# Local-attention layers of a decoder: another order of steps within each head-pair slot, on four engines

## The chip, the cores and the metric

The program runs on 1 core of one Trainium2 chip. The metric is the device time of one execution, in microseconds. Five engines work on it, each through its own list of instructions in order, and wait for one another by semaphores: TensorE (PE in the rows; PEld is its weight load), VectorE (DVE), ScalarE (ACT), GpSimd (POOL) and SyncE (SP), which here only issues DMAs.

## The reference, cut to what matters

The program is a decoder of many sublayers on x of 4 x 512 x 128. The change touches the last sublayer alone, six layers of local attention with a gated feed-forward part, in float32:

```python
for i in range(DEPTH):                                   # 6
    x = attn_layer(shift_tokens(x), Wqkv[i], ...) + x    # 16 heads of 64
    x = ffn_layer(shift_tokens(x), ln_g[i], ...) + x
# attn_layer
q = l2norm(q) * qs; k = l2norm(k) * ksc                  # per head
q = q * cos * scale + rotate_half(q) * sin * scale       # k likewise with 1/scale
out = local_attention(q, k, v)     # window 32: own block and the one before, masked softmax
return out.reshape(b, n, INNER) @ Wo
# ffn_layer
xn = (x - mu) / jnp.sqrt(var + 1e-05) * g + bln
a, gate = jnp.split(xn @ W1 + b1, 2, -1)
return a * gelu(gate) @ W2 + b2
```

## The kernel before, in words

The function is `local_attention_layers_3`. It walks through 6 layers x 4 batch rows = 24 batches, and each batch through 8 pairs of heads (`hp` 0 to 7): 192 **slots**. A slot with number n is one turn of the loop in each engine's `batch`. All loops are unrolled, and what stands in the four `batch` functions is the order in which each engine works; no scheduler moves it. The slots are pipelined: in slot n an engine works on pairs n+2, n+1, n and n-1 at different stages.

The stages of one pair m, with the functions that do them:

- `qk` (PE, L3031): queries and keys of 512 tokens, 8 matmuls, in two halves j = 0 and 1 into banks 0 and 3. The first half waits until ScalarE is done with the first head's exponentials (`exps`) two pairs earlier, since bank 0 also holds that head's scores.
- `square_part` (ACT, L3232), a half each; then `rotate` (DVE, L3363 and L3366) on the same half, which waits for that half's square; `norms` (DVE, L3375), `floor_norms` (DVE), `inverse_norms` (ACT, L3238 Ln and L3241 Exp), `add_parts` (POOL, L2975), `normalise` (DVE, L3395).
- `turn_qk` (PE, L3047 and L3050): transposes of the normalised queries (bank 6) and keys (bank 7); `copy_qT` and `copy_kT` (ACT, L3251 and L3255) take them to SBUF.
- `direct` (PE, L3076 and L3084): the mask and the scores, into banks 0 (first head) and 2 (second head). It waits for both copies, for the previous pair's exponentials, and for the square and the rotation of the half of the following pair that lies in bank 0.
- `maxima` (DVE, L3403), `exps` (ACT, L3263, 8 activations with sums into `loc_by_query`), `inverse_sums` (DVE, L3388), `divide_probs` (POOL, L2982).
- `turn_probs` (PE, L3063 and L3064): transposes of the probabilities into banks 4 and 5. It waits for `divide_probs`, and until VectorE has taken the previous pair's output out of the same banks (`heads_out`, L3411). `exps` of the next pair waits until `turn_probs` has read `loc_by_query`.
- `project_v` (PE, L3039) and `copy_v` (ACT, L3247); `copy_probs` (ACT, L3273); `values` (PE, L3105), the output of the pair in banks 4 and 5.

The feed-forward part of batch k-1 is spread over the slots of batch k. On PE it stands at the end of a slot: `project_out` in slots 0 and 1 (4 matmuls of 512 columns each time, L3115), `turn_shifted` in 2, `turn_z` in 3, `hidden` for the gate in 4 and for the other half in 5 (3 matmuls each, L3138), `feed_back` in 6 (3 matmuls, L3146). ScalarE's and VectorE's steps (`add_out`, `lower_middle`, `copy_tokens`, `token_stats`, `normal_tokens`, `copy_z`, `gelus` with two table loads, `gated`, `new_state`) stand at the end of their slots too, except `normal_tokens`. PE's steps use banks 7, 6 and 1 beside the pair's own work; before `turn_qk` PE waits, in slots 1 to 7, for the step that frees such a bank.

Of the kernel before, what the change touches and what calls it, by code (L numbers as in the profile page):

```python
# [2839 lines left out]
def local_attention_layers_3(nc, g, io):  # L2840
# [17 lines left out]
    with ExitStack() as stack:  # L2858
# [68 lines left out]
        with nc.Block() as block:  # L2927
# [43 lines left out]
            def _(pool):  # L2971
# [31 lines left out]
                def batch(k, f):  # L3003
                    for hp in range(HP):
                        n = k * HP + hp
                        if hp == LAST:
                            by_block(k + 2)
                        prepare(n + 2)
                        divide_probs(n + 1)
                        if hp == 2 and f is not None:  # L3010
                            inverse_spread(f)
# [4 lines left out]
                divide_probs(0)  # L3016
# [6 lines left out]
            def _(pe):  # L3023
# [126 lines left out]
                def batch(k, f):  # L3150
# [3 lines left out]
                    for hp in range(HP):  # L3154
# [7 lines left out]
                        qk(n + 2, next_qk, 1)  # L3162
                        if f is not None and hp == 1:
                            pe.wait_ge(s["y_half_done"], f + 1)
# [4 lines left out]
                        if f is not None and hp == 4:  # L3169
                            pe.wait_ge(s["zT_copied"], f + 1)  # L3170
                        if f is not None and hp == 5:
                            pe.wait_ge(s["gelu_done"], f * NC + NC)
                        if f is not None and hp == 6:
                            pe.wait_ge(s["inner_done"], f * NC + NC)
                        if f is not None and hp == LAST:
                            pe.wait_ge(s["y_done"], f + 2)
                        turn_qk(n + 1)
                        turn_probs(n)
                        if hp == LAST:
                            pe.wait_ge(s["xv_done"], k + 2)  # L3180
                        project_v(n + 1, next_v)
                        direct(n + 1)
                        values(n, u)
                        if f is not None:
# [4 lines left out]
                            if hp == 3:  # L3189
                                turn_z(f)  # L3190
                            if hp == 4:
# [3 lines left out]
                            if hp == 5:  # L3195
                                pe.wait_ge(s["v_copied"], n + 2)
                                hidden(f, A_BANKS, 0, "a_ready")
                            if hp == 6:
# [16 lines left out]
                f = BATCHES - 1  # L3215
                pe.wait_ge(s["v_copied"], BATCHES * HP + 1)
# [4 lines left out]
                turn_z(f)  # L3221
                hidden(f, GATE_BANKS, INNER, "gate_ready")
# [5 lines left out]
            def _(act):  # L3228
# [6 lines left out]
                def inverse_norms(m, j):  # L3235
                    part = slice(8 * j, 8 * j + 8)
                    act.wait_ge(s["floored_done"], m * 2 + (j + 1))
                    nc.scalar.activation(norm_log[:, part], floored[:, part], ACT.Ln).then_inc(s["norm_log_done"], 1)  # L3238
                    act.wait_ge(s["norm_log_done"], m * 2 + (j + 1))
                    when(act, "rotated_done", m * 2 + (j - 1))  # L3240
                    nc.scalar.activation(inv_norm[:, part], norm_log[:, part], ACT.Exp,  # L3241
                                         scale=-0.5).then_inc(s["inverse_done"], 1)
# [14 lines left out]
                def exps(m):  # L3257
                    when(act, "probs_turned", m * 2)
                    for h in range(2):
                        act.wait_ge(s["max_done"], m * 2 + (h + 1))  # L3260
                        for t in range(QT):
                            r, at = t // 2, (t % 2) * 2 + t // 2
                            nc.scalar.activation(by_query[:, h, :, t % 2, r, :],  # L3263
                                                 score_banks[h][:, t * 2 * BLOCK:(t + 1) * 2 * BLOCK].rearrange(
                                                     "p (w k) -> p w k", w=2), ACT.Exp,
                                                 bias=minus_max[:, t, h:h + 1],
# [448 lines left out]
```

## Time and profile before

| what | value |
|---|---|
| three runs | 5072.9, 5081.94 and 5083.23 us, median 5081.94 |
| the profiled execution's own time | 5055.95 us |
| its span, first to last instruction | 5054.2 us |
| granted TensorE clock, mean | 0.836 of full |
| local layers: first `qk` matmul | at 3010.7 us |
| DVE busy in them, 4000 to 4100 us | 79.5 of 100 us |
| ACT, PE, POOL busy there | 77.0, 86.1, 51.9 of 100 us |

The page gives the busy time of each engine over the whole span (PE 3786.9 us, DVE 3245.7, ACT 2783.0, POOL 1469.9). For the change only the last two fifths count, from about 3010 us on. The way to read them is slot by slot: which instruction waits, for whom, and whether that one was working or waiting itself. The last chain that the page prints covers only the closing transposes after the local layers.

### The profile page before, as it was taken

What the parts mean: (1) busy time and instruction counts of PE and PEld (TensorE: products, weight loads), DVE (VectorE), ACT (ScalarE), POOL (GpSimd) and SP (SyncE); (2) the same over time, 40 slices, a digit from 0 to 9 for tenths busy, and PEclk for the clock granted to TensorE, in tenths of its full rate; (3) what the DMA queues carried; (4) which work ended last, traced back from release to release, by engine and by line L of the source; (5) the groups of instructions that cost most, each with busy time, mean ns of one, the idle gap of its engine ahead of it and who ended that gap; (6) DMA issues with size and microseconds to landing.
All of it is one profiled execution on the core that took longest, in us unless ns stands there. A gap on an engine that the chain in (4) does not pass through costs nothing. (4 is left out here: it accounts for less than half of the span.)

```text
span 5054.2 us, 96137 instructions
## 1 busy us (share of the span) xinstructions
PE 3786.9 (75%) x32669; PEld 2234.6 (44%) x32898; DVE 3245.7 (64%) x6512; ACT 2783.0 (55%) x7830; POOL 1469.9 (29%) x2402
## 2 busy tenths in 40 slices
PE   2004767995758995886996668888888888888886
PEld 1003333333342222443442336666666666666664
DVE  8996445444328786425555328778777878787775
ACT  2034623442536785441224438777777777777775
POOL 0011202331111111110001235545454545454453
PEclk6556877556778987887997779999999999999998
DMA  1001123102114310203450000000000000000000
GB/s 45 0 0 33 35 76 68 42 11 41 27 34 101 78 27 12 59 10 96 137 140 25 1 24 29 5 9 24 5 28 5 9 24 5 9 24 5 28 5 11
DMA packets 139048, 170.17 MB, mean 34 GB/s; under 512 B 34607, under 2 KB 121755, under 8 KB 137412
## 3 DMA queue, kind: packets, MB, share of 16 engines
q1 hardware_dynamic: 138158, 164.06, 13.4%
q8 instruction: 260, 4.26, 0.4%
q14 instruction: 198, 1.62, 0.1%
q0 software_dynamic: 432, 0.23, 0.0%
HBM read 124.06 MB, written 32.89 MB: 31 GB/s over the span
## 5 line engine op out<-in xcount | busy, mean ns | idle before, releaser
L854 DVE TENSOR_REDUCE minus_max<-banks 128x1 f32<-128x512 f32 (+4 forms) x1152 | 622.0, 572 | 452.9 <-PE banks L664 440.9
L771 ACT ACTIVATE probs<-banks 128x512 f32<-128x512 f32 (+4 forms) x1152 | 613.8, 559 | 406.8 <-PE banks L632 397.4
L2982 POOL TENSOR_TENSOR loc_by_query<-loc_by_query,loc_inv_sums 128x512 f32<-128x512 f32 x386 | 469.6, 1235 | 559.5 <-DVE loc_inv_sums L3388 559.5
L2975 POOL TENSOR_TENSOR loc_cos_part<-loc_cos_part,loc_sin_part 128x512 f32<-128x512 f32 x388 | 487.8, 1276 | 412.9 <-DVE loc_sin_part L3366 412.3
L3263 ACT ACTIVATE loc_by_query<-banks,loc_minus_max 128x128 f32<-128x128 f32 x1544 | 540.5, 374 | 13.2 <-DVE loc_minus_max L3403 12.7
L3031 PE MATMUL banks<-loc_w_qkv,loc_shifted 128*128 128x256 f32 x1552 | 410.9, 412 | 169.4 <-ACT loc_by_query L3263 155.7
L632 PE MATMUL banks<-q_stack,k_stack 51*128 51x512 bf16 (+4 forms) x1152 | 438.9, 427 | 39.3 <-DMA q_stack<-max_rows 37.2
L664 PE MATMUL banks<-k_stack,q_stack 48*128 48x512 bf16 (+5 forms) x1536 | 437.1, 346 | 30.1 <-PEq L68 19.4
L3031 PEld LDWEIGHTS banks<-loc_w_qkv,loc_shifted 128*128 128x128 f32 x1552 | 307.9, 204 | 282.2 <-issue 230.0
L705 PE MATMUL banks<-probs,pair_rows 128*32 128x256 f32 (+1 forms) x4352 | 396.9, 446 | 9.5 <-issue 9.3
L3363 DVE TENSOR_TENSOR loc_cos_part<-banks,loc_table 128x512 f32<-128x512 f32 x388 | 265.3, 684 | 126.2 <-ACT loc_square L3232 125.2
L3263 ACT ACTIVATION_READ_ACCUMULATOR loc_by_query<-banks,loc_minus_max 128x1 f32 x1544 | 331.2, 215 | 0.0
L1365 ACT ACTIVATE gated<-banks 128x512 f32<-128x512 f32 x168 | 100.3, 597 | 336.2 <-PE banks L1326 336.2
L3232 ACT ACTIVATE loc_square<-banks 128x512 f32<-128x512 f32 x388 | 225.2, 604 | 106.8 <-PE banks L3031 106.1
L2028 PE MATMUL banks<-identity,srt_b 128*128 128x128 f32 x64 | 11.2, 320 | 344.6 <-DVE srt_b L2299 344.6
L3395 DVE TENSOR_TENSOR loc_rotated<-loc_cos_part,loc_inv_norm 128x512 f32<-128x512 f32 x388 | 267.2, 689 | 1.1 <-issue 0.6
L206 POOL TENSOR_SCALAR fin_shifted<-fin_moments 128x4 f32<-128x4 f32 x48 | 12.0, 249 | 870.4 <-DVE fin_moments L306 868.0
L3366 DVE TENSOR_TENSOR loc_sin_part<-banks,loc_table 128x512 f32<-128x512 f32 x388 | 264.0, 681 | 0.0
L3375 DVE TENSOR_REDUCE loc_norm_sq<-loc_square 128x8 f32<-128x512 f32 x388 | 246.1, 676 | 0.0
L1385 DVE TENSOR_TENSOR product<-gated,banks 128x512 f32<-128x512 f32 x168 | 115.7, 689 | 199.0 <-PE banks L1328 198.9
L632 PEld LDWEIGHTS banks<-q_stack,k_stack 51*128 51x128 bf16 (+1 forms) x1152 | 101.2, 97 | 284.1 <-issue 112.0
L3388 DVE RECIPROCAL loc_inv_sums<-loc_sums 128x4 f32<-128x4 f32 x386 | 68.7, 178 | 235.4 <-ACT loc_by_query L3263 235.4
(492 smaller groups left out, 8711.8 us busy)
## 6 DMA issues: line engine op xcount, KB each, us to landing
expert_share<-limited_rows SPq DMA_DIRECT2D x136, 256.0 KB, 4.1
expert_w<-in_L_ffn_pairs_dram SPq DMA_DIRECT2D x84, 192.0 KB, 2.4
q_stack<-q_pieces SPq DMA_DIRECT2D x38, 384.0 KB, 6.4
loc_w_qkv<-in_L_ffn_Wqkv_dram SPq DMA_DIRECT2D x7, 1536.0 KB, 8.0
expert_share<-grouped_rows SPq DMA_DIRECT2D x32, 256.0 KB, 4.0
k_stack<-k_pieces SPq DMA_DIRECT2D x20, 384.0 KB, 9.0
q_pieces<-q_parts SPq DMA_DIRECT2D x19, 384.0 KB, 2.6
q_stack<-max_rows SPq DMA_DIRECT2D x384, 3.0 KB
```

The source lines that it names most:

```text
L632: nc.tensor.matmul(t_bank(n, k, e)[:, q0:S], k_stack[rows_e, k0:k0 + P], q_stack[rows_e, q0:S], start=not mask, stop=True, skip_group_chec ...
L664: ins = nc.tensor.matmul(d_bank(n, k, i)[:, at * nk:at * nk + keys], q_stack[rows_e, q * P:(q + 1) * P], k_stack[rows_e, 0:keys], start=pl ...
L705: ins = nc.tensor.matmul(o_bank[at:at + COLS, lo:hi], pair_rows[quad % 2][u][:, k, e, :], probs_of(2 * quad + u, k, e)[:, lo:hi], start=(k ...
L771: nc.scalar.activation(probs_of(n, k, e)[0:kn, q0:S], t_bank(n, k, e)[0:kn, q0:S], ACT.Exp, scale=scale).then_inc(s["exp_done"], 1)
L854: nc.vector.tensor_reduce(minus_max[:, n % 2, 1 - i, qs[0]:qs[0] + len(qs)], view, AX.X, ALU.max, negate=True).then_inc(s["max_done"], 1)
L2975: nc.gpsimd.tensor_tensor(cos_part[:, tiles, :], cos_part[:, tiles, :], sin_part[:, tiles, :], ALU.add).then_inc(s["summed"], 1)
L2982: nc.gpsimd.tensor_tensor(seen, seen, inv_sums[:, h, :].unsqueeze(1).unsqueeze(3).to_broadcast([P, 2, QT, BLOCK]), ALU.mult).then_inc(s["p ...
L3031: ins = nc.tensor.matmul(g.bank[3 * j][:, (t % 2) * QK:(t % 2 + 1) * QK], xs[:, t * P:(t + 1) * P], w_qkv[:, ds(at, QK)], start=True, stop ...
L3263: nc.scalar.activation(by_query[:, h, :, t % 2, r, :], score_banks[h][:, t * 2 * BLOCK:(t + 1) * 2 * BLOCK].rearrange("p (w k) -> p w k", ...
L3363: nc.vector.tensor_tensor(cos_part[:, tiles, :], g.bank[3 * j][:, :].rearrange("p (t d) -> p t d", t=2), table[:, 0, tiles, :], ALU.mult). ...
L3366: nc.vector.tensor_tensor(sin_part[:, tiles, :].rearrange("p t (e two d) -> p (t e) two d", two=2, d=half), src, table[:, 1, tiles, :].rea ...
L3395: nc.vector.tensor_tensor(groups(rotated[:, tiles, :]), groups(cos_part[:, tiles, :]), inv_norm[:, part].unsqueeze(2).to_broadcast([P, 8, ...
```

## The change

Each engine's `batch` gets another order, and some helpers are cut differently:

- PE: `project_v(n+1)` moves ahead of the waits and of `turn_qk(n+1)`; `values` works on pair n-1 and stands ahead of `direct(n+1)`; `turn_probs(n)` stands behind `direct(n+1)`, at the end of the pair's work. The feed-forward steps from `turn_z` on move one slot later, and the waits before `turn_qk` with them.
- ACT: the slot begins with `copy_probs(n-1)`; the second half's square moves behind `copy_qT` and `copy_kT` (in slot 6 it stands ahead of `gelus`); `exps` is called for each head alone, with one `inverse_norms` on all 16 columns between the two, in place of two on 8 columns each. `copy_tokens`, `copy_z` and `gelus` stand between the first square and `copy_qT` in slots 3, 5 and 6.
- DVE: the slot begins with `inverse_sums(n, 0)`, both `normalise(n+1)` and `inverse_sums(n, 1)`; then `rotate(n+2)`, the first `norms`, `heads_out(n-1)`, the first head's `maxima(n+1)`, the second `norms`, one `floor_norms` on 16 columns in place of two, and the second head's `maxima`. `add_out`, `normal_tokens` and `new_state` stand behind `normalise`, `gated` ahead of it, `token_stats` and the tables of the next layer at the end of the slot.
- POOL: `divide_probs(n)` stands ahead of `prepare(n+2)`; before it was `divide_probs(n+1)` behind it.

The core of the diff (PE and the two engines' loops):

```diff
                         qk(n + 2, next_qk, 0)
                         qk(n + 2, next_qk, 1)
+                        if hp == LAST:
+                            pe.wait_ge(s["xv_done"], k + 2)
+                        if f is not None and hp == 6:
+                            pe.wait_ge(s["gelu_done"], f * NC + 1)
+                        if f is not None and hp == LAST:
+                            pe.wait_ge(s["inner_done"], f * NC + 1)
+                        project_v(n + 1, next_v)
...
                         turn_qk(n + 1)
+                        if n > 0:
+                            values(n - 1, 1 - u)
+                        direct(n + 1)
                         turn_probs(n)
-                        if hp == LAST:
-                            pe.wait_ge(s["xv_done"], k + 2)
-                        project_v(n + 1, next_v)
-                        direct(n + 1)
-                        values(n, u)
...
-                            if hp == 4:
+                            if hp == 5:
                                 pe.wait_ge(s["pack_loaded"], (f // B) * 16 + 16)
                                 pe.wait_ge(s["v_copied"], n + 2)
                                 hidden(f, GATE_BANKS, INNER, "gate_ready")
...
+                        if n > 0:
+                            copy_probs(n - 1)
                         square_part(n + 2, 0)
-                        square_part(n + 2, 1)
+                        if f is not None and hp == 3:
+                            copy_tokens(f)
+                        if f is not None and hp == 5:
+                            copy_z(f)
+                        if f is not None and hp == 6:
+                            square_part(n + 2, 1)
+                            gelus(f)
                         copy_qT(n + 1)
                         copy_kT(n + 1)
-                        copy_probs(n)
+                        if f is None or hp != 6:
+                            square_part(n + 2, 1)
                         copy_v(n + 1, 1 - u)
...
-                        inverse_norms(n + 2, 0)
-                        inverse_norms(n + 2, 1)
-                        exps(n + 1)
...
+                        exps(n + 1, 0)
+                        inverse_norms(n + 2)
+                        exps(n + 1, 1)
```

**ScalarE, one slot of batch 0, before.** `loc_square` is the square of a half, `loc_by_query` the exponentials, `loc_probs` the turned probabilities' copy.

```order
L3263 ACTIVATE loc_by_query,loc_sums<-banks,loc_minus_max 128x2x64 x8
L3232 ACTIVATE loc_square<-banks 128x512 x2
L3251 ACTIVATE loc_qT<-banks 128x512
L3255 ACTIVATE loc_kT<-banks 128x512
L3273 ACTIVATE loc_probs<-banks 128x384 x2
L3247 ACTIVATE loc_v_1<-banks 128x512
```

The same engine and slot now:

```order
L3266 ACTIVATE loc_by_query,loc_sums<-banks,loc_minus_max 128x2x64 x4
L3276 ACTIVATE loc_probs<-banks 128x384 x2
L3238 ACTIVATE loc_square<-banks 128x512
L3255 ACTIVATE loc_qT<-banks 128x512
L3259 ACTIVATE loc_kT<-banks 128x512
L3238 ACTIVATE loc_square<-banks 128x512
L3251 ACTIVATE loc_v_1<-banks 128x512
```

The second square moved from ahead of the two copies of turned queries and keys to behind them.

**VectorE, one slot of batch 0, before.**

```order
L3411 COPY loc_headsT<-banks 128x512
L3363 TENSOR_TENSOR loc_cos_part<-banks,loc_table 128x512
L3366 TENSOR_TENSOR loc_sin_part<-banks,loc_table 128x512
L3363 TENSOR_TENSOR loc_cos_part<-banks,loc_table 128x512
L3366 TENSOR_TENSOR loc_sin_part<-banks,loc_table 128x512
L3375 TENSOR_REDUCE loc_norm_sq<-loc_square 128x8 x2
L3382 TENSOR_SCALAR loc_floored<-loc_norm_sq 128x8 x2
L3403 TENSOR_REDUCE loc_minus_max<-banks 128x4 x2
L3395 TENSOR_TENSOR loc_rotated<-loc_cos_part,loc_inv_norm 128x512
```

The same engine and slot now:

```order
L3367 TENSOR_TENSOR loc_cos_part<-banks,loc_table 128x512
L3370 TENSOR_TENSOR loc_sin_part<-banks,loc_table 128x512
L3367 TENSOR_TENSOR loc_cos_part<-banks,loc_table 128x512
L3370 TENSOR_TENSOR loc_sin_part<-banks,loc_table 128x512
L3379 TENSOR_REDUCE loc_norm_sq<-loc_square 128x8
L3412 COPY loc_headsT<-banks 128x512
L3404 TENSOR_REDUCE loc_minus_max<-banks 128x4
L3379 TENSOR_REDUCE loc_norm_sq<-loc_square 128x8
L3385 TENSOR_SCALAR loc_floored<-loc_norm_sq 128x16
L3404 TENSOR_REDUCE loc_minus_max<-banks 128x4
```

The copy of the heads' output moved from ahead of the rotations to right ahead of the first maxima.

**TensorE, from the transposes of queries and keys to the next slot's `qk`, now** (before, the same rows stood in the order `loc_rotated`, `loc_by_query`, `loc_by_block`, band and `loc_kT`, `loc_probs`):

```order
L3030 MATMUL banks<-loc_w_qkv,loc_shifted 128x256 x4
L3038 MATMUL banks<-loc_w_qkv,loc_by_block 128x128 x4
L3046 MATMUL banks<-identity,loc_rotated 128x128 x4
L3049 MATMUL banks<-identity,loc_rotated 128x128 x4
L3104 MATMUL banks<-loc_probs,loc_v_1 64x96 x12
L3104 MATMUL banks<-loc_probs,loc_v_1 64x64 x4
L3104 MATMUL banks<-loc_probs,loc_v_edge_1 64x32 x2
L3075 MATMUL banks<-loc_band_direct,identity_bf 128x512 x2
L3083 MATMUL banks<-loc_kT,loc_qT 64x96 x16
L3062 MATMUL banks<-identity,loc_by_query 128x2x64
```

The turned probabilities (last row) moved from ahead of the scores to behind them, and the values from behind the scores to ahead of them.

## Rows read from the trace of the kernel before

**Rows 1.** Busy time by stretch: start:end, length, then each engine's busy us
```profile
4000.00:4100.00 100.00, 86.14 (x1059) 67.06 (x1068) 79.52 (x172) 76.96 (x284) 51.90 (x44) 0.98 0.04 11
```
**Rows 2.** Summary of L3276 from 3050 us on: count, ns, first and last start
```profile
L3276 ACT ACTIVATE loc_shifted<-loc_yT x24: 617/641/642, 3078.8 to 4974.0; 64x512 f32<-64x512 f32 x24
```
**Rows 3.** Timeline of DVE: start us, us, engine line, tiles [idle before it <-releaser]
```profile
3066.55 0.18 DVE L3388 RECIPROCAL loc_inv_sums<-loc_sums 128x4 f32<-128x4 f32 x1 [0.60 <-ACT loc_by_query L3263]
...
3073.46 0.18 DVE L3388 RECIPROCAL loc_inv_sums<-loc_sums 128x4 f32<-128x4 f32 x1 [0.57 <-ACT loc_by_query L3263]
...
3074.86 0.18 DVE L3388 RECIPROCAL loc_inv_sums<-loc_sums 128x4 f32<-128x4 f32 x1 [0.60 <-ACT loc_by_query L3263]
...
3075.53 0.68 DVE L3363 TENSOR_TENSOR loc_cos_part<-banks,loc_table 128x512 f32<-128x512 f32 x1
...
3077.92 1.27 DVE L3375 TENSOR_REDUCE loc_norm_sq<-loc_square 128x8 f32<-128x512 f32 x2
```
**Rows 4.** Timeline of ACT in the same slot
```profile
3071.24 0.21 ACT L3238 ACTIVATE loc_norm_log<-loc_floored 128x8 f32<-128x8 f32 x1 [0.66 <-DVE loc_floored L3382]
...
3071.94 0.35 ACT L3263 ACTIVATE loc_by_query<-banks,loc_minus_max 128x128 f32<-128x128 f32 x1
...
3074.71 0.60 ACT L3232 ACTIVATE loc_square<-banks 128x512 f32<-128x512 f32 x1
```
**Rows 5.** Timeline of PE in the same slot
```profile
3073.57 1.97 PE L3031 MATMUL banks<-loc_w_qkv,loc_shifted 128*128 128x256 f32 x8 [1.67 <-ACT loc_by_query L3263]
3075.37 0.60 PE L3047 MATMUL banks<-identity,loc_rotated 128*128 128x128 f32 x4
...
3077.20 1.06 PE L3039 MATMUL banks<-loc_w_qkv,loc_by_block 128*128 128x128 f32 x8
```
**Rows 6.** Timeline where PE's turned probabilities wait for the heads' copy
```profile
3379.54 0.66 DVE L3411 COPY loc_headsT<-banks 128x512 f32<-128x512 f32 x1
...
3380.26 0.33 PE L3063 MATMUL banks<-identity,loc_by_query 128*128 128x128 f32 x1 [0.92 <-DVE loc_headsT L3411]
```
**Rows 7.** Timeline from a gelu step to the next slot, ACT, DVE and PE
```profile
3976.72 1.28 ACT L3294 ACT_TABLE_LOAD   x1
3978.01 1.83 ACT L3298 ACTIVATE loc_gate<-banks,loc_pack 85x512 f32<-85x512 f32 x3
...
3981.16 1.09 ACT L3232 ACTIVATE loc_square<-banks 128x512 f32<-128x512 f32 x2
...
3995.19 0.60 ACT L3251 ACTIVATE loc_qT<-banks 128x512 f32<-128x512 f32 x1 [1.58 <-PE banks L3047]
3995.68 0.59 ACT L3255 ACTIVATE loc_kT<-banks 128x512 f32<-128x512 f32 x1
...
3981.79 0.69 DVE L3363 TENSOR_TENSOR loc_cos_part<-banks,loc_table 128x512 f32<-128x512 f32 x1 [4.29 <-ACT loc_square L3232]
...
3994.50 0.66 PE L3047 MATMUL banks<-identity,loc_rotated 128*128 128x128 f32 x4 [1.52 <-DVE loc_inner L3457]
```
**Rows 8.** Timeline of PE's feed-forward steps and the `qk` behind one
```profile
3187.87 3.70 PE L3115 MATMUL banks<-loc_headsT,loc_w_o 128*128 128x512 f32 x8
...
3973.71 2.81 PE L3138 MATMUL banks<-loc_zT,loc_pack 128*85 128x512 f32 x6
3976.35 1.89 PE L3031 MATMUL banks<-loc_w_qkv,loc_shifted 128*128 128x256 f32 x8
```
**Rows 9.** Timeline of ACT's two feed-forward copies out of bank 7
```profile
3955.72 0.63 ACT L3284 ACTIVATE loc_mid_tokens<-banks 128x512 f32<-128x512 f32 x1
...
3966.64 0.81 ACT L3290 ACTIVATE loc_zT<-banks,loc_pack 128x512 f32<-128x512 f32 x1
```
**Rows 10.** A stretch of PE alone: busy us, granted clock, DMA share, GB/s
```profile
3180.00:3184.00 4.00, 4.00 (x16) 0.57 0.00 0
```
**Rows 11.** Timeline of PE there
```profile
3179.70 2.91 PE L3031 MATMUL banks<-loc_w_qkv,loc_shifted 128*128 128x256 f32 x8 [1.88 <-ACT loc_by_query L3263]
3182.41 1.06 PE L3047 MATMUL banks<-identity,loc_rotated 128*128 128x128 f32 x4
```

More of the change, by code:

```diff
@@ L3347, in _ @@
                 f = BATCHES - 1
+                copy_probs(BATCHES * HP - 1)
                 lower_middle(f)
@@ L3469, in batch @@
                         n = k * HP + hp
-                        if not isinstance(n, int) or n > 0:
+                        inverse_sums(n, 0)
+                        if f is not None and hp == LAST:
+                            gated(f)
+                        normalise(n + 1, 0)
+                        normalise(n + 1, 1)
+                        if k > 1 and hp == 0:
+                            new_state(k - 2)
+                        if f is not None and hp in (1, 2):
+                            add_out(f, hp - 1)
+                        if f is not None and hp == 4:
+                            normal_tokens(f)
+                        inverse_sums(n, 1)
+                        rotate(n + 2, 0)
+                        rotate(n + 2, 1)
+                        norms(n + 2, 0)
+                        if n > 0:
                             before = (hp - 1) % HP
                             if hp == 0:
-                                parts = None if k_minus(k, 2) is None else (k - 1) * 2
+                                parts = (k - 1) * 2 if k > 1 else None
                             else:
@@ L3476, in batch @@
                             heads_out(n - 1, before, parts)
-                        rotate(n + 2, 0)
-                        rotate(n + 2, 1)
-                        norms(n + 2, 0)
+                        maxima(n + 1, 0)
                         norms(n + 2, 1)
+                        floor_norms(n + 2)
+                        maxima(n + 1, 1)
+                        if f is not None and hp == 3:
+                            token_stats(f)
                         if hp == 5:
@@ L3484, in batch @@
                                 tables(new_layer)
-                        if f is not None and hp == 3:
-                            normal_tokens(f)
-                        floor_norms(n + 2, 0)
-                        floor_norms(n + 2, 1)
-                        maxima(n + 1)
-                        normalise(n + 2, 0)
-                        inverse_sums(n + 1, 0)
-                        normalise(n + 2, 1)
-                        inverse_sums(n + 1, 1)
-                        if f is None:
-                            continue
-                        if hp < 2:
-                            add_out(f, hp)
-                        if hp == 2:
-                            token_stats(f)
-                        if hp == 5:
-                            gated(f)
-                        if hp == 6:
-                            new_state(f)
-                def k_minus(k, count):
-                    return None if isinstance(k, int) and k < count else k
                 dve.sem_inc(s["y_done"], 1)
```

121 lines of the change are left out of this document (53 added, 68 removed).

## The prediction

> **What bounds the kernel now.** I first read the busy time of a stretch of the local layers [rows 1]: VectorE works 79.5 of 100 us, ScalarE 77.0, and TensorE's 86.1 holds overlapping records. No engine is full, so the order of the waits sets the time. The summary of the one activation that runs once per batch gives the batch's price: 24 starts from 3078.8 to 4974.0 us, (4974.0 - 3078.8) / 23 = 82.4 us per batch of 8 slots [rows 2]. Then the timelines of a plain slot (batch 0, no feed-forward). It takes 74.86 - 66.55 = 8.31 us, and VectorE idles in it only 0.57 and 0.60 us, both times behind the exponentials [rows 3]. So now the loop is: VectorE without a gap from the heads' copy to the maxima, ScalarE's exponentials (start 71.94, the square behind them at 74.71: 2.77 us, [rows 4]), then VectorE again. The other 82.4 - 66.5 = 15.9 us of a batch are feed-forward steps that stick out: PE's long steps more than fill its 1.67 us wait before `qk` [rows 5, 8], and the gelus hold VectorE for 4.29 us [rows 7].
>
> **The change, part by part: the plain slot.** I follow what each first instruction waits for, from the first head's maxima (time 0) to the same point one slot later.
>
> 1. The heads' copy stands directly ahead of the maxima and ends at about 0.08 (it starts 0.60 earlier and lasts 0.66). `turn_probs`, now behind `direct`, waits for it and starts 0.06 later, as it did at 3380.26 [rows 6]: 0.14.
> 2. `exps` of the first head overwrites what the first four transposes read. Four transposes reach ScalarE 0.69 us after their start (3994.50 to 3995.19, [rows 7]), 0.06 more for the slow first record [rows 6]: `exps` starts at 0.89. The maxima alone would have allowed 0.60.
> 3. `qk` of the next slot starts 1.63 us behind the first exponential (71.94 to 73.57, [rows 4, 5]): 2.52.
> 4. `qk` occupies PE 1.80 (73.57 to 75.37), `project_v` 0.90 (record 1.06, its end overlaps the next) [rows 5], then `turn_qk` 0.69 to `copy_qT`, which starts at 5.91. The normalised halves are done by about 4.0, so PE's own order sets this.
> 5. `copy_qT` to `copy_kT` 0.49 [rows 7], `copy_kT` to the second square 0.48 (the same size), square to rotation 0.63 (3981.16 to 3981.79, [rows 7]): the second rotation starts at 7.51.
> 6. Rotation 1.20 (four operations take 77.92 - 75.53 = 2.39, [rows 3]), first `norms` 0.60, heads' copy 0.60: the next first maxima start at 9.91.
>
> So the slot costs **9.91 us where it costs 8.31 now**. The loop is the second square: ahead of the copies it depended on `qk` alone; behind them it waits for the whole of PE's `project_v` and transposes, and VectorE cannot pass the rotation that waits for it. What is saved (two small ScalarE operations of 0.35 together between 71.24 and 71.94, one floor, VectorE's 1.17 us of waits) lies beside this loop and gives nothing. ScalarE alone would need, from `exps`: 2.77, inverse norms 0.35, copy of probabilities 0.75, four operations at 0.48, then 0.15 + 2.40: about 9.2 with the 0.89 ahead.
>
> **The slots with feed-forward work.** From the start of `qk` at q, the period is q + 1.80 + 0.90 + 0.69 + 0.49 + 0.48 + 0.63 + 2.40 = q + 7.39. PE ends `turn_probs` at 1.07 and does its step before `qk`.
> - Behind slots 0 and 1, `project_out` takes 3.53 (3.70 less the overlap, [rows 8]): q = 4.60, **11.99** each. VectorE's additions wait for it and fit before the rotation (6.3).
> - Behind 2, `turn_shifted` (0.6) ends ahead of 2.52. But `copy_tokens` (0.63, [rows 9]) stands behind the first square (at 4.75 to 5.23), and PE waits for it: `turn_qk` at 5.90 and not 5.22, **10.59**.
> - Behind 3: `token_stats` (1.4) and the GpSimd inverse end at 4.85, `normal_tokens` (1.24) at 6.1, the second rotation at 7.5 as before: **9.91**.
> - Behind 4: `copy_z` takes 0.81 [rows 9], `turn_qk` at 6.08: **10.77**.
> - Behind 5, three matmuls of `hidden` take 2.64 (73.71 to 76.35, [rows 8]): q = 3.71. In slot 6 the second square stands early (5.7), then a table load 1.29, the gelus 1.86, another load 1.29 [rows 7]: `copy_qT` at 10.65, `copy_kT` ends at 11.75, `direct` 1.26: **13.06**.
> - Behind 6, `turn_probs` needs no wait, q = 3.33: **10.72**. Behind 7 `feed_back` takes 2.68: **11.14**. `gated` and `new_state` are hidden in VectorE's idle time.
>
> Sum: 11.99 + 11.99 + 10.59 + 9.91 + 10.77 + 13.06 + 10.72 + 11.14 = 90.17 us per batch, against 82.4. The tables of the next layer now fall beside other work; that is inside these figures.
>
> **The clock.** The granted clock is at its full level (2.4 GHz) for most of these layers. It fell to the lower one (0.57 mean from 3180 to 3184, so mostly 1.2 GHz) after PE had idled 1.88 us before `qk` [rows 10, 11]. There `qk` took 2.91 us, not 1.97, and four transposes 1.06, not 0.60: 0.94 + 0.46 = 1.4 us, all on the new loop. Most plain slots of before idle 1.67 us at the same place without it [rows 5]. In the changed plain slot PE waits about 1.8 us ahead of `turn_probs`, works 0.93 and waits 1.45 again: more idle time around less work than any plain slot has now. Bounds for the extra: nothing (as most of today's) and 1.4 in each slot. I take half, 0.7 per plain slot, and 1.3 per batch with feed-forward work (0.7 in slot 3, 0.3 in the gelu slot, 0.3 in the two with short PE steps), since the long steps fill the pause in the others. The Trainium skill ("TensorE: Matmul & The Clock Gate", HAM oscillation) warns of single long gaps in the matmuls and would let pauses as short as these pass; the row above speaks against it, with 1.88 us. By the page the sum would be the case without clock loss below.
>
> **The sum** against the profiled execution (5055.95 us; the median of the three runs, 5081.94, is 26 above it, and I add that): 23 batches x (90.17 + 1.3 - 82.4 = 9.07) = 208.6; five plain slots of batch 0 before the first row of [rows 2], 5 x (9.91 + 0.7 - 8.31) = 11.5; three slots behind the last row 2; one more `copy_probs` and `values` at the end 1. Together +223: 5279 in a profile, **5305 us** as a median; I say 5303.
>
> **The rivals.**
> - *No clock loss*: 23 x 7.77 + 5 x 1.6 + 3 = +190, 5272 us. For it: today's pauses of 1.67. Chance 0.2.
> - *Clock loss in every plain and short-step slot*: 3.6 per batch, 23 x 11.4 + 5 x 3 + 3 = +280, 5362. Chance 0.15.
> - *ScalarE's own chain and not PE's sets the loop*, if `exps` and `qk` come at 0.60 and 2.0 (the transposes' read is over earlier than I think): slots of 9.1, the long ones 0.3 shorter: about 86.6 per batch, +104, 5186. Chance 0.1.
> - *Faster: the plain slot stays at 8.31 and the feed-forward steps vanish.* It needs the second square no later than today's, so the loop 1.6 us shorter than I sum. Then a batch is 8 x 8.31 + 2 x 1.9 (what `project_out` exceeds PE's pause by) + 3 x 1.0 + 3 for the gelus = 76.3, 23 x -6.1 = -140, 4942 us. For it: VectorE's work in a slot is only 8.31 - 1.17 = 7.1 us. Against it: the copies ahead of the square wait for PE by the order of the lists. Chance 0.05.
> - *The change moves nothing*: the two effects cancel at 82.4 per batch. 0.01.
>
> The forecast has 0.49. The range takes in the cases with and without clock loss, 5210 to 5362; most of the two fast rivals and a part of the slowest stay out. A measurement of this kernel can tell about 0.2%, 10 us, from no change. Chances: faster 0.05, same 0.01, slower 0.94.
>
> **What would show it.** Plain slots of batch 0 between 9.7 and 11.3 us apart; VectorE idle ahead of `loc_cos_part` behind ScalarE's square, ScalarE idle ahead of `loc_qT` behind PE's transposes; more stretches of PE at the lower clock; starts of L3276's successor 90 to 93 us apart. The forecast is wrong if VectorE's long wait is elsewhere, if plain slots stay near 8.3, or if PE finds its inputs late at `values` or `direct`.

## The result, and the profile after

| | before | changed |
|---|---|---|
| median of four runs | 5077.42 us | 5290.25 us |
| lowest and highest | 5068.91, 5083.23 | 5273.44, 5317.42 |
| profiled execution, span | 5054.2 us | 5284.9 us |

The ratio is 1.043, with a 95% interval of 1.0402 to 1.0458: the change makes the kernel 4.3% slower, 213 us. The forecast was 5303 us.

The stretch that answers to [rows 1], of the changed kernel: every engine works less per 100 us (VectorE 73.2 and not 79.5, ScalarE 65.9 and not 77.0). Scaled to one batch, which takes 91.2 us and not 82.4 (next row), that is an estimate of 66.7 us of VectorE's work where it was 65.5, and 60.1 us of ScalarE's where it was 63.4. So hardly any work was added; the engines wait longer.

```profile
4000.00:4100.00 100.00, 81.16 (x932) 61.99 (x932) 73.17 (x143) 65.93 (x235) 43.04 (x39) 0.97 0.02 4
```

The activation that runs once per batch, which answers to [rows 2]; its line is now L3279. (5195.7 - 3098.0) / 23 = 91.2 us per batch, against 82.4:

```profile
L3279 ACT ACTIVATE loc_shifted<-loc_yT x24: 627/629/630, 3098.0 to 5195.7; 64x512 f32<-64x512 f32 x24
```

In the list of costliest groups of the changed kernel, three waits carry the story. Their last two columns are the idle time right before the group and what ended it:

```profile
L3266 ACT ACTIVATE loc_by_query<-banks,loc_minus_max 128x128 f32<-128x128 f32 x1544 | 542.0, 363 | 502.7 <-PE banks L3063 461.5
...
L3367 DVE TENSOR_TENSOR loc_cos_part<-banks,loc_table 128x512 f32<-128x512 f32 x388 | 264.9, 683 | 306.5 <-ACT loc_square L3238 303.6
...
L3062 PE MATMUL banks<-identity,loc_by_query 128*128 128x128 f32 x768 | 193.5, 291 | 240.8 <-DVE loc_headsT L3412 240.8
```

VectorE waits 303.6 us for ScalarE's squares (125.2 on the page of before). TensorE's turned probabilities wait 240.8 us for VectorE's copy of the heads, and ScalarE's exponentials wait 461.5 us for the turned probabilities. One loop shows itself at three places.

A plain slot (batch 0) of the changed kernel shows it in order. First VectorE, which answers to [rows 3]; columns as there:

```profile
3074.57 0.69 DVE L3367 TENSOR_TENSOR loc_cos_part<-banks,loc_table 128x512 f32<-128x512 f32 x1 [0.46 <-ACT loc_square L3238]
3075.18 0.68 DVE L3370 TENSOR_TENSOR loc_sin_part<-banks,loc_table 128x512 f32<-128x512 f32 x1
3076.63 0.69 DVE L3367 TENSOR_TENSOR loc_cos_part<-banks,loc_table 128x512 f32<-128x512 f32 x1 [0.77 <-ACT loc_square L3238]
...
3078.43 0.68 DVE L3412 COPY loc_headsT<-banks 128x512 f32<-128x512 f32 x1
3079.03 0.55 DVE L3404 TENSOR_REDUCE loc_minus_max<-banks 128x4 f32<-128x384 f32 x1
```

Then ScalarE in the same slot, which answers to [rows 4, 7]:

```profile
3073.92 0.63 ACT L3238 ACTIVATE loc_square<-banks 128x512 f32<-128x512 f32 x1
3075.03 0.60 ACT L3255 ACTIVATE loc_qT<-banks 128x512 f32<-128x512 f32 x1 [0.48 <-PE banks L3046]
3075.52 0.59 ACT L3259 ACTIVATE loc_kT<-banks 128x512 f32<-128x512 f32 x1
3076.00 0.60 ACT L3238 ACTIVATE loc_square<-banks 128x512 f32<-128x512 f32 x1
...
3079.86 0.37 ACT L3266 ACTIVATE loc_by_query<-banks,loc_minus_max 128x128 f32<-128x128 f32 x1 [2.77 <-PE banks L3063]
```

And TensorE, which answers to [rows 5, 6]. A float32 matmul of the program leaves two records, so x8 are the 4 matmuls of `qk`; a transpose leaves one:

```profile
3071.70 1.97 PE L3030 MATMUL banks<-loc_w_qkv,loc_shifted 128*128 128x256 f32 x8 [1.25 <-ACT loc_by_query L3266]
...
3074.39 0.60 PE L3046 MATMUL banks<-identity,loc_rotated 128*128 128x128 f32 x4
...
3079.17 0.33 PE L3062 MATMUL banks<-identity,loc_by_query 128*128 128x128 f32 x1 [1.50 <-DVE loc_headsT L3412]
...
3081.51 0.77 PE L3030 MATMUL banks<-loc_w_qkv,loc_shifted 128*128 128x256 f32 x1 [1.25 <-ACT loc_by_query L3266]
```

Read across the three (starts are given without their 3000): `copy_qT` waits for the transposes (0.48), the second square stands behind both copies (76.00), the second rotation waits for it (0.77, start 76.63), the heads' copy and the maxima follow without a gap (79.03), the transposes of probabilities wait for that copy (79.17), the exponentials for the transposes (79.86), `qk` for the exponentials (81.51). TensorE pauses twice, 1.50 and 1.25 us.

The starts of the first head's maxima give the length of each step. All the slots of one kind agree to 0.02 us unless the clock falls in them or just ahead of them, so the clean value (of steps at 2.4 GHz) stands beside the forecast. The means are over all batches, and for the plain slots over the 8 steps from slot 0 of batch 0:

| from slot to slot | forecast | clean | mean |
|---|---|---|---|
| plain (batch 0) | 9.91 | 9.81 | 10.76 |
| 0 to 1, 1 to 2 (`project_out`) | 11.99 | 11.76 | 11.76 |
| 2 to 3 (`copy_tokens`) | 10.59 | 10.56 | 10.56 |
| 3 to 4 (`token_stats`, `normal_tokens`) | 9.91 | 10.69 | 10.84 |
| 4 to 5 (`copy_z`) | 10.77 | 10.74 | 10.85 |
| 5 to 6 (gelus) | 13.06 | 13.33 | 13.97 |
| 6 to 7 | 10.72 | 10.63 | 10.63 |
| 7 to 0 | 11.14 | 10.91 | 10.91 |
| batch | 90.17 | 90.37 | 91.26 |

From slot 0 to the last such start of the whole stage it is 2174.6 us, and 1959.6 us before: 215 us. This length, which I call the stage, is what I compare below, beside the ratios. It is read from one profiled execution of each kernel. It leaves out the sublayers ahead, whose end differs by up to 39 us between executions of kernels that are the same there (first `qk` at 3005.7 to 3044.2 us). The stretches at 1.2 GHz (low stretches below) are counted over the same length: 26 with 89 us in all before, 32 with 113 us in the changed kernel.

### The profile page after: what moved, and what is told of

Same layout as the page of the kernel before. It is cut to its first block and busy times, and to the rows that moved or that the text cites. A ratio compares the mean times of both kernels' runs of the same rounds, so it can differ in the third digit from the quotient of the medians.

```text
span 5284.9 us, 95795 instructions
## 1 busy us (share of the span) xinstructions
PE 3882.9 (73%) x32898; PEld 2262.0 (43%) x32898; DVE 3321.3 (63%) x6314; ACT 2699.9 (51%) x7442; POOL 1417.2 (27%) x2400
## 5 line engine op out<-in xcount | busy, mean ns | idle before, releaser
L3266 ACT ACTIVATE loc_by_query<-banks,loc_minus_max 128x128 f32<-128x128 f32 x1544 | 542.0, 363 | 502.7 <-PE banks L3063 461.5
L2982 POOL TENSOR_TENSOR loc_by_query<-loc_by_query,loc_inv_sums 128x512 f32<-128x512 f32 x384 | 401.4, 1045 | 799.3 <-DVE loc_inv_sums L3390 799.3
L3367 DVE TENSOR_TENSOR loc_cos_part<-banks,loc_table 128x512 f32<-128x512 f32 x388 | 264.9, 683 | 306.5 <-ACT loc_square L3238 303.6
L3030 PE MATMUL banks<-loc_w_qkv,loc_shifted 128*128 128x256 f32 x1552 | 391.5, 397 | 88.4 <-ACT loc_by_query L3266 74.6
L3397 DVE TENSOR_TENSOR loc_rotated<-loc_cos_part,loc_inv_norm 128x512 f32<-128x512 f32 x386 | 357.5, 965 | 33.6 <-ACT loc_inv_norm L3246 33.3
L3062 PE MATMUL banks<-identity,loc_by_query 128*128 128x128 f32 x768 | 193.5, 291 | 240.8 <-DVE loc_headsT L3412 240.8
L3266 ACT ACTIVATION_READ_ACCUMULATOR loc_by_query<-banks,loc_minus_max 128x1 f32 x1544 | 312.5, 202 | 0.0
L2028 PE MATMUL banks<-identity,srt_b 128*128 128x128 f32 x64 | 11.8, 331 | 344.5 <-DVE srt_b L2299 344.5
L3379 DVE TENSOR_REDUCE loc_norm_sq<-loc_square 128x8 f32<-128x512 f32 x388 | 261.6, 675 | 0.0
L3238 ACT ACTIVATE loc_square<-banks 128x512 f32<-128x512 f32 x388 | 236.8, 610 | 48.3 <-PE banks L3030 48.3
L3038 PE MATMUL banks<-loc_w_qkv,loc_by_block 128*128 128x128 f32 x1544 | 214.5, 284 | 61.7 <-ACT loc_gate L3301 61.7
L3038 PEld LDWEIGHTS banks<-loc_w_qkv,loc_by_block 128*128 128x128 f32 x1544 | 209.6, 199 | 80.8 <-ACT loc_gate L3301 70.9
```

The lines of the kernel that those rows point to most:

```text
L2982: nc.gpsimd.tensor_tensor(seen, seen, inv_sums[:, h, :].unsqueeze(1).unsqueeze(3).to_broadcast([P, 2, QT, BLOCK]), ALU.mult).then_inc(s["p ...
L3030: ins = nc.tensor.matmul(g.bank[3 * j][:, (t % 2) * QK:(t % 2 + 1) * QK], xs[:, t * P:(t + 1) * P], w_qkv[:, ds(at, QK)], start=True, stop ...
L3038: ins = nc.tensor.matmul(g.bank[1][:, j * P:(j + 1) * P], xv[:, j * P:(j + 1) * P], w_qkv[:, ds(at + QK, P)], start=True, stop=True)
L3266: nc.scalar.activation(by_query[:, h, :, t % 2, r, :], score_banks[h][:, t * 2 * BLOCK:(t + 1) * 2 * BLOCK].rearrange("p (w k) -> p w k", ...
L3367: nc.vector.tensor_tensor(cos_part[:, tiles, :], g.bank[3 * j][:, :].rearrange("p (t d) -> p t d", t=2), table[:, 0, tiles, :], ALU.mult). ...
L3397: nc.vector.tensor_tensor(groups(rotated[:, tiles, :]), groups(cos_part[:, tiles, :]), inv_norm[:, part].unsqueeze(2).to_broadcast([P, 8, ...
```

## The experiments

**1. The square alone, undone.** Of the changed kernel, ScalarE's second square goes back ahead of the two copies; all the rest of the change stays.

```diff
                         square_part(n + 2, 0)
+                        square_part(n + 2, 1)
...
-                            square_part(n + 2, 1)
                             gelus(f)
                         copy_qT(n + 1)
                         copy_kT(n + 1)
-                        if f is None or hp != 6:
-                            square_part(n + 2, 1)
```

> The changed kernel with one part undone: ScalarE's second square stands ahead of copy_qT and copy_kT again. Theory (the loop runs through the second square): the plain slot falls from 9.81 us to about 9.0 (first maxima at 0, copy of probabilities ends at 4.75, first square to rotation 0.63, rotations 2.40, norms and heads' copy 1.20), slots behind project_out from 11.76 to about 10.5, the batch from 91.3 to about 84, the whole to about 5110 us. Rival (the late turned probabilities or the late values set the loop, the square only waits beside them): plain slots stay within 0.2 us of 9.81 and the time above 5240 us.

Measured: 5089.83 us, ratio to before 1.0049 (1.0026 to 1.0072). The stage takes 1980.8 us and not 2174.6, the plain slot 8.96 us, the slots behind `project_out` 10.19, the batch 83.39. VectorE's timeline of a plain slot of this kernel:

```profile
3068.41 0.69 DVE L3365 TENSOR_TENSOR loc_cos_part<-banks,loc_table 128x512 f32<-128x512 f32 x1 [0.46 <-ACT loc_square L3238]
3069.01 0.68 DVE L3368 TENSOR_TENSOR loc_sin_part<-banks,loc_table 128x512 f32<-128x512 f32 x1
3069.61 0.68 DVE L3365 TENSOR_TENSOR loc_cos_part<-banks,loc_table 128x512 f32<-128x512 f32 x1
3070.21 0.68 DVE L3368 TENSOR_TENSOR loc_sin_part<-banks,loc_table 128x512 f32<-128x512 f32 x1
```

The second wait is gone and the first is left, 0.46 us as it was. 194 of the 215 us go with this one instruction's place. The rival (the late values or probabilities hold the slot) falls: they are as late here as in the changed kernel.

**2. The same part alone, done to the kernel before.**

```diff
-                        square_part(n + 2, 1)
                         copy_qT(n + 1)
                         copy_kT(n + 1)
+                        square_part(n + 2, 1)
```

> The kernel before with that part alone done: ScalarE's second square moved behind copy_qT and copy_kT, nothing else. Theory: in a plain slot the second rotation starts 0.94 us later (77.66 and not 76.72 in the timeline of before), so it takes about 9.25 us and not 8.31, and the whole about 165 us more, 5242 us. Rival (the square is harmless by itself, it takes the moved values and scores to hurt): under 5110 us.

Measured: 5186.75 us, ratio 1.0241 (1.0208 to 1.0274), stage 2075.2 us: 116 more than before. The plain slot at the full clock takes 9.18 us (9.25 expected), but six of the eight of batch 0 take 10.6 to 11.8, and the stage holds 53 stretches at 1.2 GHz (218 us) where the kernel before has 26 (89 us). VectorE now waits 2.08 us for that square in a slot with a low clock:

```profile
3069.46 0.69 DVE L3363 TENSOR_TENSOR loc_cos_part<-banks,loc_table 128x512 f32<-128x512 f32 x1 [2.08 <-ACT loc_square L3232]
```

TensorE's `qk` in the same slot took 3.40 us and not the 1.97 of [rows 5], after a pause of 2.54:

```profile
3063.73 3.40 PE L3031 MATMUL banks<-loc_w_qkv,loc_shifted 128*128 128x256 f32 x8 [2.54 <-ACT loc_by_query L3263]
```

I had expected 165 us, from 0.94 us in every slot. In the slots with feed-forward work the square often hid behind a longer wait (from 9.95 to 9.95 us in the first, 10.92 and 10.92 in the third), so less than that was lost there, and the clock took the difference back in part. The part is harmful alone, and costs more (194 us) inside the new order. In a plain slot at the full clock the price is the same in both orders: 9.18 - 8.31 = 0.87 us here, 9.81 - 8.96 = 0.85 us there. The difference lies in the slots with feed-forward work: behind `project_out` the late square costs 11.76 - 10.19 = 1.57 us each time in the new order, and nothing in the old one.

**3. The pauses filled.** The changed kernel with matmuls that nothing uses: 4 of 512 columns ahead of `turn_probs` in all slots but the gelu slot, 8 ahead of the wait for the gelus.

```diff
                         direct(n + 1)
+                        if f is None or hp != 6:
+                            fill(6, 4)
                         turn_probs(n)
...
                         if f is not None and hp == 6:
+                            pe.wait_ge(s["exp_done"], (n + 1) * 2 * QT)
+                            fill(2, 8)
                             pe.wait_ge(s["gelu_done"], f * NC + 1)
```

> The changed kernel with work added that nothing uses: 4 matmuls of 512 columns in bf16 (about 0.85 us) ahead of turn_probs in every slot but the gelu slot, and 8 of them ahead of the wait for the gelus, all in TensorE's idle time. Theory (the idle stretches cost clock): the 11.1 to 11.5 us slots of batch 0 fall to 9.81, the gelu slots from 14.1 to 13.3, nearly no stretch at 1.2 GHz is left in these layers, and the whole is about 29 us shorter than the changed kernel, 5261 us. Rival (those slots are long for another reason): they stay, and the time stays at 5290 or rises.

Measured: 5265.54 us, ratio 1.0408 (1.0374 to 1.0441). The intervals of this ratio and of the changed kernel's overlap, so the slots decide: the stage is 22 us shorter (2152.6), the low stretches fall from 32 (113 us) to 5 (17 us), the gelu step is 13.33 us in the mean too (13.97 in the changed kernel), the mean batch 90.52 against a clean 90.37. In batch 0 the long slots are gone but for two of 11.50. TensorE's timeline there; the row with x4 is the filling, and the pause after it is 0.53 where it was 1.50:

```profile
3072.99 1.04 PE L3110 MATMUL banks<-loc_band_direct,identity_bf 128*128 128x512 bf16 x4
3074.56 0.33 PE L3062 MATMUL banks<-identity,loc_by_query 128*128 128x128 f32 x1 [0.53 <-DVE loc_headsT L3420]
```

So more work on TensorE made these layers shorter in the profiled execution, and the steps that got shorter are those in which the clock no longer fell. What the falls cost in the changed kernel is about these 22 us, a tenth of the loss; that the whole kernel is shorter, its four runs don't settle.

**4. Two buffers of probabilities**, so that `exps` overwrites nothing that `turn_probs` still reads.

```diff
-        by_query = sbuf("loc_by_query", [P, 2, 2, QT // 2, 2, BLOCK])
+        by_queries = [sbuf(f"loc_by_query{u}", [P, 2, 2, QT // 2, 2, BLOCK]) for u in range(2)]
...
-                    when(act, "probs_turned", (m - 1) * 2 + h + 1)
+                    by_query = by_queries[m % 2]
+                    when(act, "probs_turned", (m - 2) * 2 + h + 1)
```

> The changed kernel with two buffers of probabilities, so that exps doesn't wait until turn_probs has read the last pair's. Theory: exps follows the maxima at 0.62 and not at 0.83 to 0.89 us, plain slots fall by about 0.25 us to 9.55; slots with a long TensorE step don't change, since TensorE sets them; about 14 us in all, 5276 us. Rival (the probabilities' order is what holds the slots): 0.25 us or more in every slot, 50 us or more in all.

Measured: 5273.26 us, ratio 1.0412 (1.0361 to 1.0463), which by itself can't be told from the changed kernel. In the stage: 15.5 us less. The plain slot is 9.63 us (-0.18, 0.25 expected), the steps 2 to 3 and 4 to 5 also lose 0.18, those behind `project_out`, `hidden` and `feed_back` nothing. These 54 steps make 9.7 us; the rest goes with the clock, whose low stretches are 27 here and not 32. ScalarE's wait of 2.77 us for the transposes has become one of 2.58 us for the maxima. That wait of 461.5 us in the list, the largest of the local layers, was thus worth 0.18 us in plain slots and in two of eight others: it stood for the loop, not for its cause.

```profile
3066.44 0.37 ACT L3269 ACTIVATE loc_by_query<-banks,loc_minus_max 128x128 f32<-128x128 f32 x1 [2.58 <-DVE loc_minus_max L3407]
```

**5. The next loop.** With the square ahead, 8.96 us is the chain exponentials, copy of the probabilities, first square, rotations. This kernel takes experiments 1 and 4 and puts `copy_probs` behind the squares in plain slots and in slots 3 to 5.

```diff
+                        late = f is None or hp in (3, 4, 5)
-                        if n > 0:
+                        if n > 0 and not late:
                             copy_probs(n - 1)
                         square_part(n + 2, 0)
...
+                        if n > 0 and late:
+                            copy_probs(n - 1)
                         copy_qT(n + 1)
```

> The changed kernel with the second square ahead of the copies (as in e1_square_ahead), two buffers of probabilities (as in e4_two_buffers), and copy_probs behind the squares in plain slots and in slots 3 to 5. Theory (with the square ahead, the next loop is ScalarE's: exponentials, copy of probabilities, first square, rotation, 8.96 us): plain slots fall from 8.96 to about 8.3 us, where TensorE's order qk, project_v, turn_qk, values, direct gives 8.2; slots 2 and 4 lose 0.4 to 0.5 us, slot 3 and the slots behind a long TensorE step stay; the whole is about 5064 us. Rival (VectorE's own work sets the 8.96): plain slots stay above 8.8 us and the time at 5085 or more.

Measured: 5055.06 us, ratio 0.997 (0.9948 to 0.9992), stage 1939.7 us. The plain slot is 8.34 us, near the 8.2 to 8.3 of the expectation, so the rival (VectorE's own work sets the 8.96) falls. That TensorE's list is what sets the 8.34 is argued from that sum, not shown. It equals the 8.31 of before: in none of the kernels tried here does the new order bring anything in a plain slot. The gain is in the feed-forward slots, 81.8 us per batch against 82.6.

**6 and 7. Tokens, table, filling.** Of experiment 5, `normal_tokens` behind the rotations of slot 4, and the table load behind the gelus put behind the copies of slot 6; in 7 the 8 filling matmuls of experiment 3 as well.

```diff
-                        if f is not None and hp == 4:
-                            normal_tokens(f)
                         inverse_sums(n, 1)
                         rotate(n + 2, 0)
                         rotate(n + 2, 1)
+                        if f is not None and hp == 4:
+                            normal_tokens(f)
...
                         copy_v(n + 1, 1 - u)
+                        if f is not None and hp == 6:
+                            nc.scalar.preload_act_table_set("natural_log_exp_and_others")
```

> As e5_probs_late, with normal_tokens behind the rotations of slot 4 (VectorE idled 1.0 us ahead of it, and it took 1.75 us and not 1.24 beside GpSimd's division), and the table load behind the gelus put behind the copies of slot 6. Theory: the step from slot 3 to 4 falls from 10.7 to about 9.7 us, the gelu slot by 1.3 us, about 53 us in all, 5011 us. Rival for the table (the copies need the table, a load stays ahead of them): the gelu slot doesn't change and the time is near 5040.

Measured: 5061.91 us, ratio 0.9977 (0.9961 to 0.9993), stage 1946.5: a miss, 7 us more than experiment 5 and not 53 less (the intervals of the two ratios overlap). The step from slot 3 to 4 rose from 10.7 to 11.18 us, and the mean of the next one from 9.40 to 9.73. VectorE's and then GpSimd's timeline of this kernel show why:

```profile
3304.31 3.24 DVE L3456 TENSOR_SCALAR loc_z<-loc_mid_tokens,loc_moments,loc_rstd 128x128 f32<-128x128 f32 x4
```

```profile
3304.73 2.48 POOL L2975 TENSOR_TENSOR loc_cos_part<-loc_cos_part,loc_sin_part 128x512 f32<-128x512 f32 x2
```

Four operations, which take 0.33 us each where GpSimd is idle, took 3.24 us: the second and the third lasted 1.31 and 1.30 us and ended 0.09 us behind GpSimd's first and second addition. The table load did move, but brought 0.57 us of the 1.3 (clean gelu step 12.49, from 13.06): what is late next there was not tried; by the order of the lists it is TensorE's `project_v` and transposes, which wait for the gelus.

> As e6_tokens_table, with 8 matmuls of 512 columns in bf16 that nothing uses, ahead of TensorE's wait for the gelus. Theory: the gelu slots lose the 0.8 us that a stretch at 1.2 GHz costs them in two of three batches, about 13 us in all, 4998 us. Rival (the extra matmuls hold up project_v): no shorter than e6_tokens_table.

Measured: 5062.32 us, ratio 0.9958 (0.994 to 0.9977), stage 1941.2. The gelu step is 12.49 to 12.50 in all batches (mean 13.18 without the filling), 0.7 us as expected; but a low stretch now falls between slots 4 and 5 of all 23 batches with feed-forward work, where experiment 6 had it in 12; the mean step from 4 to 5 rises from 9.73 to 10.18, and that takes most of it back: 5 us of the stage and not 13, and no gain that the medians show.

**8. `normal_tokens` where GpSimd is idle**, behind the first maxima of slot 4; all else as in 7.

```diff
                         maxima(n + 1, 0)
+                        if f is not None and hp == 4:
+                            normal_tokens(f)
                         norms(n + 2, 1)
```

> As e7_all_fill, but normal_tokens stands behind the first head's maxima of slot 4 and not behind the rotations, where it took 3.24 us for four small operations beside GpSimd's additions. Theory (VectorE waits for GpSimd when both read SBUF): there GpSimd is idle, the four take 1.24 us, the step from slot 3 to 4 falls from 11.2 to about 8.6 us, the next one rises by 0.5; about 2.1 us per batch, 48 us in all, near 5010 us. Rival (the four operations are slow by themselves at this place): they take over 3 us again and the time stays.

Measured: 4994.74 us, ratio 0.9841 (0.9813 to 0.987), stage 1876.1 us. This beats both kernels, by 1.6% and by 5.6%. The step from 3 to 4 is 8.34 us (11.18 before it), the one from 4 to 5 10.2, the batch 79.06. The rows of VectorE, and of GpSimd, whose additions end at 3335.93 there:

```profile
3335.02 1.76 DVE L3462 TENSOR_SCALAR loc_z<-loc_mid_tokens,loc_moments,loc_rstd 128x128 f32<-128x128 f32 x4
```

```profile
3333.43 2.50 POOL L2975 TENSOR_TENSOR loc_cos_part<-loc_cos_part,loc_sin_part 128x512 f32<-128x512 f32 x2
```

The four took 1.76 us and not the 1.24 expected, since the last 0.9 us of the additions still fell on them. Their place ahead of the maxima is free now, which is why the step lost 2.84 us, more than the four operations gained. And no stretch at 1.2 GHz is left in the stage, where experiment 7 had 23 (82 us).

**9. The other pauses filled too**, behind `turn_probs` in plain slots and slots 2 to 4.

```diff
                         turn_probs(n)
+                        if f is None or hp in (2, 3, 4):
+                            fill(6, 4)
```

> As e8_tokens_after_maxima, with 4 matmuls of 512 columns in bf16 that nothing uses behind turn_probs in plain slots and slots 2 to 4, where TensorE waits 1.3 us for the exponentials. Theory: stretches at 1.2 GHz fall from about 25 to under 10, 0.5 us per batch, about 10 us less than e8_tokens_after_maxima. Rival (they only lengthen TensorE's list): no shorter, or longer by up to 0.3 us in these slots.

Measured: 4993.49 us, ratio 0.9854 (0.9826 to 0.9882), stage 1876.0: no difference. The expectation rested on 25 low stretches, but experiment 8 has none left between its first and last slot, and neither has this kernel, so there was nothing to win. The filling costs nothing either.

## Why the prediction was right, point by point

- *The reading of before* (dense VectorE, exponentials, VectorE again; the feed-forward steps stick out) carried: it named the place at which a later square would enter.
- *Steps 1 to 3 of the loop.* Transposes at 0.14 after the maxima's start: measured 79.17 - 79.03 = 0.14. Exponentials at 0.89: 0.83, since the four transposes were read 0.69 and not 0.75 after their start. `qk` 1.63 later: 1.65.
- *Step 4*, `qk` start to `copy_qT`: 1.80 + 0.90 + 0.69 = 3.39 forecast, 3.33 measured (`qk` 71.70 and `copy_qT` 75.03 in the slot shown). *Steps 5 and 6*: 0.49, 0.48, 0.63 and 2.40 came out exactly. 9.81 against 9.91. That it is a loop and not a chance wait is what experiments 1 and 2 showed, from both sides.
- *Slots with a long TensorE step*: 11.76 against 11.99. Two terms were mis-sized. `project_out` was put at 3.53, and it takes 3.54 in every batch of before, at the full clock, but 3.44 here: behind `values` its first record lasts 0.70 us, behind the turned probabilities 0.59, like the others. Why the neighbour matters is open. And `qk` to the maxima is 7.26, not 7.39: 7.33 as in the plain slot, less 0.07 since `qk` without a pause ahead of it is that much shorter (1.89 and not 1.97 already in [rows 5, 8]).
- *Behind slot 3* the step failed: 9.91 forecast, 10.69 measured. Two durations were taken over from before though their neighbours had changed. GpSimd's two small operations for the inverse ended at 5.2 us after the maxima and not at 4.85, and `normal_tokens` took 1.76 us and not 1.24, so the first rotation began at 7.1 and not at 6.1. VectorE then worked without a gap to the maxima: here its own work, not the square, set the slot. This is the one slot that experiment 1 left as it was (10.70).
- *The gelu slot*: 13.06 forecast, 13.33 clean. In the first such slot, counted from the maxima at 3189.68, `copy_qT` starts at 10.62 (10.65 forecast) and `copy_kT` ends at 11.71 (11.75); the term that was short is `direct`, from there to the next maxima 1.62 and not 1.26.
- *Slips of addition.* 11.75 + 1.26 gives 13.01, not 13.06. In step 1, 0.66 - 0.60 gives 0.06, not 0.08, which is what was measured. Together they move the sum by 0.2 us per batch.
- *Luck in the sum.* 90.17 forecast and 90.37 clean agree better than their terms: 0.78 too little behind slot 3 and 0.27 in the gelu slot, against 0.23 too much behind each of slots 0, 1 and 7. The clock's share was put 0.4 us per batch too high, so that 91.47 stood against 91.26.
- *The clock.* The forecast was 0.7 per plain slot and 1.3 per feed-forward batch. Measured: 0.95 and 0.9, and it lay elsewhere: 0.64 in the gelu slot alone, where TensorE pauses 2.68 us and where I had put 0.3, and 0.15 behind slot 3, where I had put 0.7. By experiment 3 the clock cost the stage about 22 us; the forecast's own share for it was 23 x 1.3 + 3.5 = 33. Here is such a gelu slot of the changed kernel: the pause, then values that take 1.41 us and not 0.84:

```profile
3288.26 1.31 PE L3038 MATMUL banks<-loc_w_qkv,loc_by_block 128*128 128x128 f32 x8 [2.68 <-ACT loc_gate L3301]
...
3291.31 1.41 PE L3104 MATMUL banks<-loc_probs,loc_v 64*64 64x96 f32 x32
```

- *The rivals.* No loss of clock: excluded by the low stretches, 32 in the stage, among them four in batch 0, whose clean slots pause 1.50 and 1.25 us. The rule on single long gaps in the Trainium skill ("TensorE: Matmul & The Clock Gate", HAM oscillation) would have had this rival come true; the trace does not agree, and the measurement decides. ScalarE's own chain: it appears as soon as the square is moved back, 8.96 us in experiment 1, where I had put it at about 9.2. The faster case needed the plain slot at 8.31 us; in experiment 5 it is 8.34, but a batch takes 81.8 us and not 76.3, so even then the order gains only 0.3%.

The sum was +223 us from the profiled execution; the spans differ by 230.7, of which the stage's start gives 9.5 (3020.3 and not 3010.7 us) that have nothing to do with the change, and the stage itself 215; the other 6 lie at its start and end.

## What to carry to other kernels

In engines that run their lists in order, ask of each moved instruction what stands ahead of it now that waits for someone else, and who waits for it; add up that ring once around, from rows of the kernel before, before counting idle time saved. A large wait in the profile (461.5 us here) can be a link of the ring whose removal gives 0.18 us, while the link that costs is a wait of 0.77 us two engines away. And a duration is only good for a forecast together with its neighbours: four small VectorE operations took 3.24 us beside GpSimd's additions and 1.24 us in the kernel before.

## What the runs showed of the hardware that I had not expected

**VectorE and GpSimd in turn.** In the changed kernel `normalise` begins when GpSimd's division is running, and its two operations take 2.04 us; in slot 3, where GpSimd had not begun, they take 1.26:

```profile
3071.99 2.04 DVE L3397 TENSOR_TENSOR loc_rotated<-loc_cos_part,loc_inv_norm 128x512 f32<-128x512 f32 x2 [0.23 <-ACT loc_inv_norm L3246]
...
3261.72 1.26 DVE L3397 TENSOR_TENSOR loc_rotated<-loc_cos_part,loc_inv_norm 128x512 f32<-128x512 f32 x2
```

```profile
3071.84 1.04 POOL L2982 TENSOR_TENSOR loc_by_query<-loc_by_query,loc_inv_sums 128x512 f32<-128x512 f32 x1 [2.29 <-DVE loc_inv_sums L3390]
```

VectorE's two take 0.78 us longer, and GpSimd's operation takes its usual 1.04. In experiment 8 `normalise` came first, by 0.04 us, and there GpSimd's division takes 1.55:

```profile
3338.17 2.13 DVE L3409 TENSOR_TENSOR loc_rotated<-loc_cos_part,loc_inv_norm 128x512 f32<-128x512 f32 x2
```

```profile
3338.21 1.55 POOL L2983 TENSOR_TENSOR loc_by_query<-loc_by_query,loc_inv_sums 128x512 f32<-128x512 f32 x1 [2.28 <-DVE loc_inv_sums L3402]
```

So whoever comes second waits. The four operations of `normal_tokens` (3.24 us in experiment 6) are held up as well. The rotations, which read a PSUM bank, keep their 0.68 beside GpSimd's additions, and the copy of the heads too. The Trainium skill ("SBUF — State Buffer", Who interferes with whom) says that a VectorE instruction with two SBUF inputs contends with a GpSimd instruction that reads SBUF, and that the later one is blocked until the earlier one is done. The `normalise` rows agree. In the changed kernel's plain slots this lay off the loop; behind slot 3 it is part of the 0.78 us, and in experiment 6 it is what made the step longer.

**More work, less time.** Matmuls that nothing uses, 4 (1.04 us in the row of experiment 3) or 8 per slot in TensorE's pauses, go with a stage that is 22 us shorter (113 us at 1.2 GHz became 17). In experiment 7, where only the pause of the gelu slot was filled, a low stretch came up in another slot and took 10 of the 16 us back.
